# The 8-expert mixture by dense products, or for its chosen pairs in 40 tiles of rows

## The reference, cut to what matters

```python
def _L1_ffn_ref(x, Wr, Wg, Wu, Wd):
    E, K = 8, 2
    probs = softmax(einsum('bsh,he->bse', x, Wr))
    topk_w, topk_idx = top_k(probs, K)
    topk_w = topk_w / sum(topk_w)
    combine = einsum('bsk,bske->bse', topk_w, one_hot(topk_idx, E))
    g = einsum('bsh,ehi->besi', x, Wg)
    u = einsum('bsh,ehi->besi', x, Wu)
    y = einsum('besi,eih->besh', silu(g) * u, Wd)
    return einsum('bse,besh->bsh', combine, y)
...
x = x + tanh(g_xattn[1]) * _L1_xattn_ref(layernorm(x), ...)   # 32 heads of 8, rotary positions
x = x + tanh(g_ffn[1])   * _L1_ffn_ref(layernorm(x), ...)     # 8 experts, 2 chosen
x = x + tanh(g_xattn[2]) * _L2_xattn_ref(layernorm(x), ...)   # 16 heads of 128, q and k normed
x = x + tanh(g_ffn[2])   * _L2_ffn_ref(layernorm(x), ...)     # 2 shared experts, 16 routed, 4 chosen
```

## Time and profile before

| | |
|---|---|
| median of 3 runs | 2890.16 us (2887.99 to 2891.98) |
| profiled execution | 2902.23 us, span 2900.3 us |
| mean granted TensorE clock over the span | 0.91 of full speed |
| busy | PE 82%, PE weight load 53%, DVE 46%, ACT 41%, POOL 37% |
| first attention | 72 to 467 us |
| first feed-forward part | 467 to 514 |
| second attention | 514 to 937 |
| 8-expert mixture | 944 to 1204.5 |
| first keys, weight preparation | 1204.5 to 1240, to 1252.4 |
| third attention | 1252.4 to 1757 |
| shared experts, 80 tiles, sums | 1758 to 2119 |
| fourth layer | to 2900 |

### The profile page before, as it was taken

One profiled execution on the slowest core, in us unless ns is written; L12 is line 12 of the kernel. 1 busy time (PEld: TensorE's weight loads), 2 busy tenths in 40 slices (PEclk: granted clock), 3 DMA queues, 4 the chain that ended last, 5 costly groups with the idle time before them and its releaser, 6 DMA issues.

```text
span 2900.3 us, 36324 instructions
## 1 busy us (share of the span) xinstructions
PE 2369.5 (82%) x11097; PEld 1530.7 (53%) x11140; DVE 1348.6 (46%) x3349; ACT 1177.1 (41%) x3878; POOL 1071.3 (37%) x1054
## 2 busy tenths in 40 slices
PE   5999999788998999989999997899858665712663
PEld 4666668566666444456665664466534333302553
DVE  2443443566665333446555542433367755820112
ACT  3444443355455121356665652233336452501111
POOL 3221110233332000234445442255524555446775
PEclk9999999999999999999999998999969877756877
DMA  9910000100000200000000003356641000003776
GB/s 348 350 61 1 1 1 1 41 1 1 1 1 17 91 1 0 1 1 1 1 3 30 13 20 117 116 96 103 99 115 63 8 8 1 8 8 72 152 150 142
DMA packets 159440, 162.77 MB, mean 56 GB/s; under 512 B 26931, under 2 KB 151107, under 8 KB 158484
## 3 DMA queue, kind: packets, MB, share of 16 engines
q1 hardware_dynamic: 127124, 119.64, 13.8%
q0 software_dynamic: 32128, 40.82, 7.9%
HBM read 81.35 MB, written 79.10 MB: 55 GB/s over the span
## 4 chain that ended last, share of the span: by engine, by line
PE 60%; DVE 14%; issue 9%; DMA 5%; ACT 5%; POOL 4%; another core or an unknown queue 1%; SPq 1%; POOLq 0%; DVEq 0%; ACTq 0%
PE ps L134 51%; DMA moe_sum<-work,weights 3%; ACT work L953 2%; PE ps L550 2%; PE ps L1113 1%; DVE xn L250 1%; PE ps L224 1%; POOL work L2919 1%; DVE n_mx L1207 1%; POOL slots L2842 1%; PE ps L411 1%; PE ps L578 1%; ACT work L635 1%; PE ps L2280 1%
## 5 line engine op out<-in xcount | busy, mean ns | idle before, releaser
L134 PE MATMUL ps<-work,weights 128*128 128x512 f32 (+4 forms) x1920 | 736.4, 521 | 16.2 <-ACT work L953 8.4
L134 PE MATMUL ps<-xn_T,weights 128*128 128x512 f32 (+5 forms) x1392 | 542.4, 527 | 29.1 <-ACT weights L2056 8.0
L134 PE MATMUL ps<-weights,work 128*128 128x126 f32 (+5 forms) x2496 | 532.2, 346 | 7.4 <-DVE weights L435 5.8
L134 PEld LDWEIGHTS ps<-work,weights 128*128 128x128 f32 (+3 forms) x1932 | 313.0, 197 | 196.5 <-issue 148.6
L134 PEld LDWEIGHTS ps<-weights,work 128*128 128x128 f32 (+2 forms) x2496 | 354.0, 195 | 42.5 <-DVE weights L435 7.2
L134 PEld LDWEIGHTS ps<-xn_T,weights 128*128 128x128 f32 (+3 forms) x1392 | 229.7, 190 | 205.7 <-issue 169.7
L720 POOL TENSOR_TENSOR work<-work,rinv 128x512 f32<-128x512 f32 x128 | 133.5, 1043 | 310.1 <-DVE rinv L670 283.8
L1232 POOL TENSOR_TENSOR work<-weights,head_sel 128x512 f32<-128x512 f32 x128 | 133.2, 1045 | 246.8 <-PE ps L134 219.2
L1182 ACT ACTIVATE work<-ps,n_negm 128x128 f32<-128x128 f32 x512 | 146.4, 370 | 141.1 <-DVE n_negm L1209 137.5
L256 POOL TENSOR_TENSOR rstd<-var,neg_half 128x4 f32<-128x4 f32 x32 | 35.3, 1103 | 429.2 <-DVE var L241 429.2
L953 ACT ACTIVATE work<-ps,n_negm 128x112 f32<-128x112 f32 (+1 forms) x512 | 152.7, 350 | 73.8 <-DVE n_negm L981 73.5
(11 more groups left out here) (311 smaller groups left out, 3804.2 us busy)
## 6 DMA issues: line engine op xcount, KB each, us to landing
f_rows<-weights SPq DMA_DIRECT2D x17, 2176.0 KB, 19.1
weights<-in_L_ffn_gate_up_proj SPq DMA_DIRECT2D x16, 768.0 KB
work<-f_rows SPq DMA_DIRECT2D x80, 136.0 KB
weights<-in_L_ffn_W SPq DMA_DIRECT2D x96, 88.0 KB
weights<-in_L_ffn_down_proj SPq DMA_DIRECT2D x16, 384.0 KB
f_sum<-weights SPq DMA_DIRECT2D x2, 2176.0 KB, 15.2
moe_sum<-weights POOLq DMA_DIRECT2D x2, 2176.0 KB
weights<-in_L_xattn_Wo SPq DMA_DIRECT2D x2, 2048.0 KB, 12.6
```

The costliest lines, as they stand in the source:

```text
L134: return nc.tensor.matmul(out, lhsT, rhs, start=start, stop=stop, skip_group_check=True)
```

## The change

`F1` becomes an object of `Routed`, with 40 tiles: 32 full ones hold 4096 pairs, and up to eight broken ones. `Dense`, `make_sel` and the bf16 identity go. Both routed mixtures share semaphores, the second counting on from the first. Of the loops of `Routed`, only the names of the weights change.

```diff
-    F1 = Dense("f1", 3, Router("f1", 3, L1E, L1K, l1_wr, WK, 0, (B3, B3)), L1F, 0, l1_wg, l1_wu, l1_wd, tile(R2, 15632, 704))
+    l1_w13 = tile(R2, 8192, KD * L1E * 2 * L1F).rearrange("p (k e n) -> p k e n", k=KD, e=L1E)
+    l1_w2 = tile(R1, 0, L1E * 2 * D).rearrange("p (e f n) -> p e f n", e=L1E, f=2)
+    F1 = Routed("f1", 3, l1_front, L1F, 40, R2, l1_front.end, tile(R2, 15104, 1280), l1_w13, l1_w2, None)
```

**Routing of groups 0 to 2** stands in bodies 1 to 3 of the second attention, with new steps for the next body's queries and keys (`rope_pe`; ACT 26 to 27 and DVE 20, 23 to 21, 24 in the same way):

```diff
-            if S.ahead and t in (19, 22):
-                if t == 19:
+            if S.ahead and t in (20, 23):
+                if t == 20:
                     done(pe, xnt_ready, S.n, 1)
+                    if S.s >= 1:
+                        done(pe, F1.r.sub_ready, S.s - 1, 0)
+                rope_qk_pe(pe, S.s + 1, 0, (t - 20) // 3)
+            early_pe(pe, S, t)
...
+    def early_pe(pe, S, t):        # early_act: 17 router_out, 20 router_exp
+        if t == 16: router_logits(pe, F1.r, r)
+        if t == 18: router_turn(pe, F1.r, r)
+        if t == 28: route_places(pe, F1, r, Y[0])
+    def early_dve(dve, S, t):
+        if t == 19: router_sub(dve, F1.r, r, early_links[r])
+        if t == 22: router_top(dve, F1.r, r, early_links[r], False)
+        if t == 26: route_choices(dve, F1, r, early_links[r])
+        if t == 29: route_slots(dve, F1, r, Y[0], early_links[r])
+    def early_pool(pool, S, t):
+        n = TB * F1.K
+        if S.new and S.s >= 1 and t >= 30:
+            route_scatter(pool, F1, S.s - 1, t - 30, t - 29)
+        if S.s >= 2 and t < n - 2:
+            route_scatter(pool, F1, S.s - 2, t + 2, t + 3)
```

**The last group's tail and routing** stand in the steps u of `first_keys_*`, each of which gets a function `beside(u)` called ahead of the step's own work (on POOL behind it):

```diff
+    def between_pe(pe, u):         # ACT: 5, 6 tail_act, 7 router_out, 9 router_exp
+        if u in (0, 1):   tail_pe_y(pe, T15, u)          # at 0 behind a wait for the map of group 2
+        if u in (4, 5):   tail_pe_xn(pe, T15, u - 4)
+        if u == 6:        router_logits(pe, F.r, r)
+        if u == 7:        router_turn(pe, F.r, r)
+        if u == 10:       route_places(pe, F, r, TP)
+        if u == 12:       route_total(pe, F, r, TP)
+    def between_dve(dve, u):
+        if u in (0, 1):   tail_dve_add(dve, T15, r, u)
+        if u == 1:        tail_dve_stats(dve, T15, r)
+        if u == 3:        tail_dve_norm(dve, T15, r, (F.written, r))
+        if u == 8:        router_sub(dve, F.r, r, early_links[r])
+        if u == 9:        router_top(...); route_choices(...)
+        if u == 11:       route_slots(dve, F, r, TP, early_links[r])
+        if u == 13:       tables(dve, F, TP)
+    def between_pool(pool, u):
+        if u == 1:        tail_pool(pool, T15)
+        if 12 <= u < 12 + n // 2:
+            route_scatter(pool, F1, NS - 1, 2 * (u - 12), 2 * (u - 12) + 2)
```

**The order of the streams.** On PE (ACT and DVE alike):

```diff
-        pe.wait_ge(in_l1f, 16 * 6)
-        run_ahead(lambda S: dense_pe(pe, S), F1, pe)
-        pe.wait_ge(in_l2x, 16 * 7)
-        wr_turn_pe(pe)
-        first_keys_pe(pe, L2)
+        pe.wait_ge(in_l2x, 16 * 5)
+        first_keys_pe(pe, L2, lambda u: between_pe(pe, u))
         wide_prep_pe(pe, L2)
         pe.wait_ge(L2.wvo_ready.sem, L2.wvo_ready.value(0, HEADS // 2 - 1))
-        pe.wait_ge(wr_ready.sem, wr_ready.value(0, 0))
+        pe.wait_ge(F1.tables_ready, 1)
+        pe.wait_ge(in_l1f, 16 * 6)
+        tiles_run(lambda g, new, old: tiles_pe(pe, F1, g, new, old), F1, pe)
+        sums1_pe(pe)
         pe.wait_ge(pool_consts, 3)
-        wide_all(wide_pe, L2, pe, lambda S, t: route_pe(pe, F2, S, t))
+        wide_all(wide_pe, L2, pe, beside_l2(lambda S, t: route_pe(pe, F2, S, t), lambda S, t: later_pe(pe, S, t)))
```

**The sums.** `sums1_*` load and add group 0's sums, norm it and turn it (and `wr_turn` stands there); those of groups 1 to 3 are added in the third attention's first body, whose own tail goes (`NO_TAIL = (4, 6)`), in four steps each (`later_*`: at the first `sum1_dve` and the power, then the norm, then two transposes and copies):

```diff
+    def sum1_dve(dve, g):
+        dve.wait_ge(sum_in[g], 32)
+        nc.vector.tensor_tensor(both[:, 0, :], both[:, 0, :], both[:, 1, :], ALU.add).then_inc(F.moved.sem, 1)
+        nc.vector.scalar_tensor_tensor(x, both[:, 0, :], gates[:, 5:6], x, ALU.mult, ALU.add).then_inc(F.moved.sem, 1)
+        tail_dve_stats(dve, n, g)
```

**Transfers.** SP writes the rows of both mixtures at the start, 28 transfers with the accumulators, and the later ones are moved. In the first "..." stand the loads of the positions, of the router's weights and of wk, wv, wo, gq and gk of the third attention; in the second the four transfers of F1's gate and up weights and the two of its down weights:

```diff
+        rows_init(sp, F1)
         rows_init(sp, F2)
         sp.wait_ge(L0.y_mm.sem, L0.y_mm.value(NS - 1, HEADS - 1))
-        sp.wait_ge(rows_zeroed, F2.row_inits)
+        sp.wait_ge(rows_zeroed, row_inits)
...
         sp.wait_ge(L1.y_mm.sem, L1.y_mm.value(NS - 1, KD - 1))
+        for x, name in enumerate(("L1_ffn_Wg", "L1_ffn_Wu")):
...
+        sp.wait_ge(F1.tables_ready, 1)
+        sp.wait_ge(L2.wvo_mm.sem, L2.wvo_mm.value(0, HEADS // 2 - 1))
+        sp.wait_ge(F1.written.sem, F1.written.end)
+        tiles_first(lambda g: tiles_sp(sp, F1, g), F1, sp)
+        sums1_sp(sp)                 # l2_wq behind the last y product, then all adds awaited, then 8 loads of sums
         prep_sp(sp)
```

More of the change, by code:

```diff
@@ L594, in wide_pe @@
                 key_tr(pe, A, s + 1, t - 1, B6)
-            if S.new and t - TAIL_T in (0, 1):
+            if S.tail and t - TAIL_T in (0, 1):
                 if A.rms and t == TAIL_T and s >= 2:
@@ L598, in wide_pe @@
                 tail_pe_y(pe, S.n, t - TAIL_T)
-            if S.new and t - TAIL_T in (4, 5):
+            if S.tail and t - TAIL_T in (4, 5):
                 tail_pe_xn(pe, S.n, t - TAIL_T - 4)
@@ L1420, in beside @@
                 rope_sin_act(act, S.s + 1)
-            if S.ahead and t == 26:
+            if S.ahead and t == 27:
                 rope_v_act(act, S.s + 1, 0, False)
+            early_act(act, S, t)
         rope_sin_act(act, 0)
@@ L1783, in _build, with __init__ @@
     blank_made = semaphore("blank_made")
-    tables_ready = semaphore("tables_ready")
     sum_in = [semaphore(f"sum_in{i}") for i in range(NS)]
     class Routed:
-        def __init__(self, name, stage, router, ff, tiles, arena, base, temp):
+        def __init__(self, name, stage, router, ff, tiles, arena, base, temp, w13, w2, last):
             R = self.r = router
@@ L1804, in __init__ @@
             self.slots_ready = signal("route_slots_ready", 1)
-            self.written = Signal(semaphore("rows_written"), 16 * TB * K, NS, 0)
+            before = last.written.end if last else 0
+            self.written = Signal(last.written.sem if last else semaphore("rows_written"), 16 * TB * K, NS, before)
             self.tot_mm = signal("route_tot_mm", 1, 1)
@@ L1880, in _build @@
     ROW_BLOCKS = 16
-    F2.row_inits = 16 * (2 + F2.rows // (ROW_BLOCKS * P))
+    row_inits = 16 * sum(2 + -(-F.rows // (ROW_BLOCKS * P)) for F in (F1, F2))
     def rows_blank(ordered):
@@ new lines, in between_pool, with sums1_sp @@
+    def between_pool(pool, u):
+        n = TB * F1.K
+        if u == 1:
+            tail_pool(pool, T15)
+        if 12 <= u < 12 + n // 2:
+            route_scatter(pool, F1, NS - 1, 2 * (u - 12), 2 * (u - 12) + 2)
+    f1_sums = (tile(WK, 0, 2048), tile(R1, 6144, 2048), tile(R2, 12288, 2048), tile(R2, 14336, 2048))
+    def sums1_sp(sp):
+        F = F1
+        sp.wait_ge(F.y_mm.sem, F.y_mm.value(F.groups - 1, TG - 1))
+        sp.dma_start(l2_wq, a["L2_xattn_Wq"].rearrange("(k p) n -> p k n", p=P)).then_inc(in_l2q, 16)
+        for i in range(2):
+            sp.wait_ge(F.added[i].sem, F.added[i].end)
+        for s in range(NS):
+            for i in range(2):
+                sum_load(sp, F, s, i, f1_sums[s])
@@ new lines, in norm1_dve, with sums1_dve, sums1_pe @@
+    def norm1_dve(dve, g):
+        n = NS * 4 + g
+        done(dve, xn_tr, n - 1, KD - 1)
+        tail_dve_norm(dve, n, g)
+    def sums1_dve(dve):
+        done(dve, y_added, T15, 1)
+        dve.sem_inc(yt_ready.sem, NS * KD)
+        dve.sem_inc(yt_tr.sem, 2 * NS)
+        dve.sem_inc(y_added.sem, 2 * NS)
+        sum1_dve(dve, 0)
+        norm1_dve(dve, 0)
+    def sums1_pe(pe):
+        done(pe, F1.y_ready, F1.groups - 1, TG - 1)
+        wr_turn_pe(pe)
+        pe.wait_ge(wr_ready.sem, wr_ready.value(0, 0))
+        for k in range(KD):
+            tail_pe_xn(pe, NS * 4, k)
+        pe.wait_ge(in_l2q, 16)
@@ new lines, in sums1_act, with sum1_at, later_pe, later_act @@
+    def sums1_act(act):
+        wr_turn_act(act)
+        for k in range(KD):
+            tail_act(act, NS * 4, 0, k)
+    def sum1_at(S, t):
+        g = (t + 3) // 4
+        if S.s != 0 or not 1 <= g < NS:
+            return None, None
+        return g, (t + 3) % 4
+    def later_pe(pe, S, t):
+        g, step = sum1_at(S, t)
+        if step in (2, 3):
+            if step == 2:
+                done(pe, xnt_ready, NS * 4 + g - 1, 1)
+            tail_pe_xn(pe, NS * 4 + g, step - 2)
+    def later_act(act, S, t):
+        g, step = sum1_at(S, t)
+        if step in (2, 3):
+            tail_act(act, NS * 4 + g, g, step - 2)
@@ L2408, in _build, with later_dve, later_pool, beside_l2 @@
+    def later_dve(dve, S, t):
+        g, step = sum1_at(S, t)
+        if step == 0:
+            sum1_dve(dve, g)
+        if step == 1:
+            norm1_dve(dve, g)
+    def later_pool(pool, S, t):
+        g, step = sum1_at(S, t)
+        if step == 0:
+            tail_pool(pool, NS * 4 + g)
+    def beside_l2(early, late):
+        def beside(S, t):
+            early(S, t)
+            late(S, t)
+        return beside
     L3H, L3HD = 16, 16
```

458 lines of the change are left out of this document (182 added, 276 removed).

## The result

The changed kernel takes 2817.66 us (median of 4 runs, 2816.29 to 2820.19) where the kernel before took 2891.07 in 4 runs beside it: a ratio of 0.9741 (95% interval 0.9725 to 0.9756), 73.4 us less. The forecast was 2812, with 2778 to 2852 as its range.

A forecast was written before the change was run, and what follows sets the result against it. PE was taken as the fullest engine, busy 82% of the span, the 8-expert stage waiting for it alone. Replaced stretch -103.5, routing +18 and sums +7 give -78.5: median 2890.2 becomes 2812 us, range 2778 to 2852.

The forecast's parts named there:

- The base: Profiled execution of the kernel before, 2902.2 us, 12.0 above the median 2890.2; the difference worked out there is taken from the median.
- the 103.5 of the replaced stretch: Second attention's last output product to third attention's first body product: 315.2 us replaced by six terms of 211.7, 103.5 less.
- Keys: Third attention's first keys with the last group's routing beside them: 35.5 + 20 us, the addition bounded by 5.4 and 31.6.
- Tiles: The 40 tiles of the new routed 8-expert stage take 111 us, like the 16-expert pass, with PE setting the pace.
- rival B: Tile pass: PE works at its low clock level, 102 us more, total 2914, slower by 24; chance 0.03.
- Rival C: Tile pass: the adds' round trip binds; at 9.1 us the gain is gone, at 12 total 2950; chance 0.03.
- Sums and next norm, 26: Behind the tiles, to the third attention's first product: 22.5 us, 1.5 for query weights ahead, 2 for slow products.
- the 2 for a slow start: Next products behind the tiles' gap start slow, after PE's granted clock of 0.50 there: 2 us more.
- Routing, +18: Second attention: routing of three groups adds 6 us a group, bounds 8.4 and 33, after the third attention's body.
- Rival A: Second attention: routing costs far more, 22 us a group, through short steps and fuller DVE; total 2860; chance 0.14.
- Sums of groups 1 to 3, +7: Third attention's first body: DVE's added sums cost some 2.3 us a group, 7 in all, bounds 0 and 13.
- First writes: 11 more 2.2 MB transfers writing the rows first end near 230 us and cost nothing, as the queues are then nearly empty.

## Why the prediction was right, and where it was not

- **The base and the 103.5 of the replaced stretch.** The mechanism held term by term, and the sum was 6.3 low in gain (109.8). *Keys*: 20 for what was put beside them, 17.2 came (52.7 against 35.5), between the bounds. "Tables and scatters fall on the same steps" was what cost: behind the loop 7.3 of the 17.2 are gone.
- **Tiles.** Taking the 16-expert pass as a measured case was worth most: 111 against 109.7. That the pass keeps the high clock is shown a second time: 0.98, which speaks against rival B. The Trainium skill (TensorE: Matmul & The Clock Gate, HAM oscillation) tells of a kernel in which PE falls back to the half rate in every round, because each round's products take less time than the wait for the next transfer. This pass isn't that case: PE is busy 106.2 of 109.7 us, so its clock says nothing against the page, and the page gives rival B no support here. Rival C is out too: POOL waited for an earlier add's landing 4 times in 40 adds, 4.4 us.
- **Sums and next norm, 26.** Right in total, wrong inside. The step "I add 1.5 (bounds 0 and 6)" failed: the weights ahead of the adds cost 4.3, since they held back the landing of the last adds and not only the sum loads' issue. The 26.1 are 9.3 to the first sum load, 5.4 to the first addition and 11.3 from there to the first product. The weights cost 2.7 more than booked; against that the 12.0 of the last part were 0.7 too large, and the 2 for a slow start stand not in this gap but behind the first product, in the third attention's body. That the total is right is luck.
- **Routing, +18.** The sum was right by luck and its layout wrong. "Bodies 2 to 4 of the second attention 6 us longer each and the first unchanged": they were 0.0, 0.2 and 7.3 longer, the first 2.5 (it had 94.1 to 99.4 in runs with the same code), and the end 7.7. Of these 17.8 us, 7.7 are the slow end, which other series don't have, and 5.6 stand in steps at a low clock, in the first and the last body. Over the seven traces that have this second attention unchanged the term is 7.5 to 17.9, each against the 398.4. The failed step is the nearest case, the third attention's body: the second's rotary steps had idle time of their own, which holds the routing, and no step of the forecast looked at how long the steps are into which the pieces go. Rival A, 22 a group, did not come.
- **Sums of groups 1 to 3, +7.** Right mechanism, size off: 11.6, within the bound of 13. The 2.3 a group were worked out for a piece that overruns its step; the steps were 3.0, 2.6 and 2.4 longer, and with the cut pieces 7.2 of the 9.3 that the 16 steps had gained are gone. The other 2.3 of the 11.6 lie between the first product and the first sum of squares, at a granted clock of 0.50 (four query products in 3.75 us at 1158.49): the slow start that the forecast had, booked in the term before.
- **First writes**: the queues are empty in the fifth and sixth slices, as forecast. The 16-expert stage and what lies behind did not move by more than the runs do among themselves.
- **The total.** The forecast was 5.7 us under the median. The three terms came to 80.4 where I had 78.5, with the errors inside them (6.3, 0.2 and 4.6) partly cancelling. The base was a trace 12 us above its median; a second trace of the kernel before was 5.8 shorter, nearly all of it behind the change, and 5.0 above its neighbour. The rest isn't explained.

## What to carry to other kernels

A piece that is put beside in-order work costs what it overruns the step it stands in: read the lengths of the steps first, put long pieces into steps that wait for something else or behind the loop, and cut the rest to what a step has free. A large load in front of a wait for small transfers holds those up as well. And read a stage's total only with its steps: two totals that agree can hide a cost and a gain of 1.7 us each, here one stretch of PE at a low clock.

## What the runs showed that I had not expected

- Eight row scatters back to back, while PE works off the last heads, go with a slow end of the stage: eight output products took 5.7 to 6.4 us in the stead of 3.70, and the end 18.7 to 19.9 in the stead of 12.2, in six traces of six from series of runs in which the kernel before takes 2891 to 2897, and in neither of the two where it takes 2872 to 2875. The cause is open.
- The rows of PE show the slow pace from 942.55 on, the engines that wait for PE stood still before: DVE was idle for 6.13 us up to 941.80, for transposes that PE's rows have done by 938.9.
- Step 5 of a body of the second attention has two lengths, 3.7 us at a granted clock of 1.00 and 5.4 at 0.66 over the stretch in it, with the same work and the same idle time ahead.
- 2 MB of weights issued 1.4 us before the last add delay its landing from 2.25 to 6.4 us.
